# Matmuls whose results nobody reads, gate scores with tokens as the moving operand, and a third normalisation done tile by tile, in a graph attention + mixture-of-experts kernel on one core

## What is computed

```python
# graph layer, on the normalised input
h   = layer_norm(node_feature, ln1_g, ln1_b)
q, k, v = (h @ Wqkv + bqkv) split, 8 heads of 64
a   = einsum(q[src], k[dst]) + dist_attn + path_attn
sa  = exp(a - segment_max(a, dst)[dst]) / segment_sum(...)[dst]
agg = segment_sum(v[src] * sa, dst)
h1  = node_feature + agg @ Wo + bo
h2  = layer_norm(h1, ln2_g, ln2_b)
x   = x + h1 + gelu(h2 @ W1 + b1) @ W2 + b2
# mixture of experts, on the third normalisation of x
xt     = layernorm(x)
shared = silu(xt @ sw1) * (xt @ sw3) @ sw2
scores = xt @ gate_w.T                      # 8 experts
idx    = top_k(scores + biases, 2);  p = sigmoid(top_k(scores, 2)) normalised
out    = x + shared + sum over the two experts of p * (silu(xt @ w1[e]) * (xt @ w3[e])) @ w2[e]
```

## Time and profile before

| | |
|---|---|
| device time, median of 3 executions | 819.65 us (819.62 to 820.09) |
| device time of the profiled execution | 819.31 us |
| its span from first to last instruction | 817.9 us |
| mean granted TensorE clock | 0.967 of full speed |
| PE busy | 758.2 us, 93% of the span |
| DVE, ACT, POOL busy | 547.0, 461.2, 221.3 us |
| DMA | 92.46 MB, mean 113 GB/s |

### The profile page before, as it was taken

One profiled execution on the slowest core, in us unless ns is written; L12 is line 12 of the kernel. 1 busy time (PEld: TensorE's weight loads), 2 busy tenths in 40 slices (PEclk: granted clock), 3 DMA queues, 4 the chain that ended last, 5 costly groups with the idle time before them and its releaser, 6 DMA issues. The chain is left out here.

```text
span 817.9 us, 13330 instructions
## 1 busy us (share of the span) xinstructions
PE 758.2 (93%) x4993; PEld 632.5 (77%) x4993; DVE 547.0 (67%) x937; ACT 461.2 (56%) x748; POOL 221.3 (27%) x156
## 2 busy tenths in 40 slices
PE   3998899999999979799999599979999999999994
PEld 2664688788878865599998499868889888888893
DVE  6637997979797844444222644357888788888855
ACT  5254686868687752733342523227667667676640
POOL 9340786868687750000000001300000000000022
PEclk9999899999999999899999689989999999999997
DMA  8231920000000007000000700956666776767214
GB/s 267 81 49 54 323 56 2 1 2 1 2 1 2 2 2 264 5 1 1 1 1 1 232 1 19 375 191 231 220 222 214 234 242 222 260 225 229 80 56 153
DMA packets 66460, 92.46 MB, mean 113 GB/s; under 512 B 6723, under 2 KB 44197, under 8 KB 65877
## 3 DMA queue, kind: packets, MB, share of 16 engines
q1 hardware_dynamic: 64149, 85.77, 32.1%
q0 software_dynamic: 2240, 5.76, 2.3%
HBM read 80.69 MB, written 10.82 MB: 112 GB/s over the span
## 5 line engine op out<-in xcount | busy, mean ns | idle before, releaser
L682 POOL TENSOR_TENSOR bias_exp_hi<-edge_exp_hi,mask 128x640 fp32r<-128x640 f32 x40 | 98.0, 2450 | 72.6 <-PE ps L828 32.3
L1806 PE MATMUL ps<-xT,w_hi 128*128 128x480 f32 (+7 forms) x512 | 111.1, 339 | 3.7 <-DVE w_lo L1621 3.6
L1806 PEld LDWEIGHTS ps<-xT,w_hi 128*128 128x128 f32 x512 | 83.2, 191 | 10.2 <-issue 3.8
L1621 DVE TENSOR_TENSOR w_lo<-weights_far,w_hi 128x1024 fp32r<-128x1024 f32 x64 | 78.0, 1219 | 3.1 <-ACT w_hi L1721 2.7
L1607 POOL DMA_INDIRECT weights_far<-slot_results,gate x5 | 5.2, 1034 | 272.2 <-DMA slot_results<-weights_near 271.0
L1808 PEld LDWEIGHTS ps<-xT,w_lo 128*128 128x128 f32 x512 | 74.0, 191 | 1.7
L1808 PE MATMUL ps<-xT,w_lo 128*128 128x240 f32 (+7 forms) x512 | 74.9, 269 | 0.0
L828 PE MATMUL ps<-onehot,bias_exp_hi 128*128 128x314 f32 x400 | 69.5, 320 | 5.5 <-POOL bias_exp_hi L682 5.0
L1721 ACT ACTIVATE w_hi<-weights_far 128x1024 fp32r<-128x1024 f32 x64 | 67.2, 1051 | 0.0
L828 PE MATMUL ps<-onehot,bias_exp_lo 128*128 128x314 f32 x400 | 65.3, 310 | 0.0
L828 PEld LDWEIGHTS ps<-onehot,bias_exp_hi 128*128 128x128 f32 x400 | 59.4, 193 | 6.5 <-POOL bias_exp_hi L682 5.2
(11 more groups left out here) (270 smaller groups left out, 1650.8 us busy)
## 6 DMA issues: line engine op xcount, KB each, us to landing
weights_far<-in_L_ffn_w SPq DMA_DIRECT2D x64, 512.0 KB, 5.4
weights_near<-in_L_ffn_w SPq DMA_DIRECT2D x32, 512.0 KB, 3.6
weights_near<-in_L_gnn_W SPq DMA_DIRECT2D x1, 4096.0 KB, 14.4
weights_near<-in_L_gnn_Wqkv SPq DMA_DIRECT2D x3, 1024.0 KB, 7.8
weights_ff<-in_L_gnn_W SPq DMA_DIRECT2D x1, 3072.0 KB, 13.3
weights_lo_shared<-in_L_ffn_sw SPq DMA_DIRECT2D x6, 512.0 KB, 7.7
weights_near<-in_L_ffn_sw SPq DMA_DIRECT2D x6, 512.0 KB, 6.3
slot_rows<-zeros SPq DMA_DIRECT2D x1, 2944.0 KB, 26.4
```

Source lines behind the costliest of these rows:

```text
L682: pool.tensor_tensor(to.rearrange("p t (h d) -> p t h d", h=H), e[:, b, :, :].unsqueeze(3).broadcast_to([P, CT, H, BN]), m.unsqueeze(2).br ...
L1621: dve.tensor_tensor(to[1], raw_rest[n] if v == V else raw[u][n], to[0], ALU.subtract)\
L1806: pe.matmul(both(bank, cap), w[u % 2][0][:, c, cut], xT(r)[:, c, :, :], start=c == 0, stop=False)
```

## The change

A helper `keep_awake` issues plain fp32 matmuls 128x512 of the identity and `iota_n` into a PSUM bank that nothing reads before it is written anew. It is called at six places of the PE stream: 3 at the end of `projections`; 3 at the start of attention (behind the load of its branch value, ahead of `sums(0, 0)`); 3 ahead of `turn(39)`, behind a wait for the 39th reciprocal; 2 and 1 ahead of feed-forward's `turn(3)` and `turn(4)`; 1 ahead of each tile's turning in the third normalisation and 2 behind the last; 4 between the experts' `turn(0)` and their first `up`.

In feed-forward the first half of the columns waits for three low parts only, the second half for all five. The gate weights are loaded and turned at the block's start. `down(14)` and `down(15)` are done for tiles 0 to 3 first and then both for tile 4. SP loads the first quarter of the shared expert's weights into `w_near` once W1 has been used. The third normalisation moves to the end of this block and goes tile by tile, the normalised row on ACT, and the high and low parts are read from PSUM. PE does the first half of `up(0)` of the shared expert there, ahead of the barrier. The routing block starts with the second half; the scores then are eight matmuls with the gate's eight columns as weights and 314 tokens moving, copied by ACT to SBUF and turned to token rows by five small matmuls in the middle of `up(1)`. The rest is passing buffers, renaming and freeing semaphores.

```diff
+def keep_awake(pe, bank, ident, filler, times):
+    for _ in range(times):
+        pe.matmul(bank[:, 0:D], ident[:, :], filler[:, 0:D], start=True, stop=True)
...
             back(2)
+            keep_awake(pe, psum[0], ident, iota_n, 3)
...
+            keep_awake(pe, psum[4], ident, iota_n, 3)
             for b in range(NB):
                 sums(b, 0)
...
                 if b:
                     turn(b - 1)
+            pe.wait_ge(inv_ready, NB - 1)
+            keep_awake(pe, psum[0], ident, iota_n, 3)
             turn(NB - 1)
             weighted_sums(NT - 1)
...
+            sp.dma_start(gate_row, gate_w).then_inc(vec_in, 16)
+            sp.dma_start(bias_r, biases.rearrange("(a n) -> a n", a=1).broadcast_to([P, EX])).then_inc(vec_in, 16)
...
+            sp.wait_ge(split_lo, 2 * MC - 1)
+            for to, frm in ((moe1, sw1[:, 0:UW].rearrange("(c p) n -> p c n", p=P)),
+                            (moe3, sw3[:, 0:UW].rearrange("(c p) n -> p c n", p=P)),
+                            (moe2, sw2[0:UW, :].rearrange("(c p) n -> p c n", p=P))):
+                sp.dma_start(to, frm).then_inc(moe_in, 16)
...
+            def moe_measure(t):
                 n = own_rows(t)
                 dve.wait_ge(y_ps, t + 1)
                 dve.tensor_tensor(xs[0:n, t, :], xs[0:n, t, :], psum[t][0:n, :], ALU.add).then_inc(y_sb, 1)
+                dve.wait_ge(y_sb, t + 1)
+                o.link(dve.bn_stats(stats[:, t, :], xs[:, t, :]))
+                dve.bn_aggr(mv[:, t, :], stats[:, t, :]).then_inc(moe_mv, 1)
+            def moe_factors(t):
+                dve.wait_ge(moe_std, t + 1)
+                o.link(dve.reciprocal(rstd[:, t:t + 1], std[:, t:t + 1]))
+                dve.scalar_tensor_tensor(out=below_mean[:, t:t + 1], in0=mv[:, t, 0:1], scalar=-1.0,
+                                         in1=rstd[:, t:t + 1], op0=ALU.mult, op1=ALU.mult).then_inc(moe_scale, 1)
+            def moe_low(t):
+                dve.wait_ge(moe_hi, t + 1)
+                cut = slice(t * P, (t + 1) * P)
+                dve.tensor_tensor(rows_T[1][:, :, cut], psum[t][:, :].rearrange("p (c n) -> p c n", c=DC),
+                                  rows_T[0][:, :, cut], ALU.subtract).then_inc(moe_lo, 1)
+            for t in range(NT):
+                moe_measure(t)
+                if t:
+                    moe_factors(t - 1)
+                if t >= 3:
+                    moe_low(t - 3)
+            moe_factors(NT - 1)
+            for t in range(2, NT):
+                moe_low(t)
...
+            for t in range(NT):
+                moe_root(t)
+                if t:
+                    moe_row(t - 1)
+                if t > 1:
+                    moe_high(t - 2)
+            moe_row(NT - 1)
+            act.preload_act_table_set("silu_and_others")
+            moe_high(NT - 2)
+            moe_high(NT - 1)
...
             def turn(t):
+                if t >= NT - 2:
+                    pe.wait_ge(columns_ready, 1)
+                    keep_awake(pe, psum[7], ident, iota_n, NT - t)
                 pe.wait_ge(rows, t + 1)
...
-            pe.wait_ge(rows_lo, NT)
...
+                    if m == 0:
+                        pe.wait_ge(rows_lo, NT if half else 3)
...
-            down(MC - 1)
+            down(MC - 2, range(NT - 1))
+            down(MC - 1, range(NT - 1))
+            down(MC - 2, range(NT - 1, NT))
+            down(MC - 1, range(NT - 1, NT))
+            pe.wait_ge(u_sb, 2 * MC)
+            for t in range(NT):
+                keep_awake(pe, psum[7], ident, iota_n, 1)
+                pe.wait_ge(moe_rows, t + 1)
+                for c in range(DC):
+                    last = pe.transpose(psum[t][:, c * P:(c + 1) * P], vs[:, t, c * P:(c + 1) * P], ident[:, :])
+                last.then_inc(moe_turned, 1)
+            keep_awake(pe, psum[7], ident, iota_n, 2)
+            pe.wait_ge(moe_lo, 3)
+            for n in range(2):
+                pe.wait_ge(moe_split_lo, n + 1)
+                for i, (wp, xp) in enumerate(passes):
+                    for c in range(DC):
+                        last = pe.matmul(up_bank[n][:, 0:SH], w1s[n][wp][:, c, :], rows_T[xp][:, c, 0:SH],
+                                         start=i == 0 and c == 0, stop=i == 2 and c == DC - 1)
+                last.then_inc(moe_a_ps, 1)
...
-            up(0)
-            for t in range(NT):
+            up(0, range(1, 2))
+            pe.wait_ge(moved, NT)
+            for half in range(2):
                 for c in range(DC):
-                    last = pe.matmul(score_ps[:, t * EX:(t + 1) * EX], hT[:, c, t * P:(t + 1) * P], gate_t[:, c, :],
+                    last = pe.matmul(psum[half][0:EX, 0:SH], gate_t[:, c, :], hT[:, c, half * SH:(half + 1) * SH],
                                      start=c == 0, stop=c == DC - 1)
-            last.then_inc(sc_ps, 1)
+            last.then_inc(sc_rows_ps, 1)
+            def scores():
+                pe.wait_ge(sc_rows_sb, 1)
+                for t in range(NT):
+                    n = own_rows(t)
+                    last = pe.transpose(score_ps[0:n, t * EX:(t + 1) * EX],
+                                        sc_rows.rearrange("e a n -> e (a n)")[:, own_cut(t)], ident[0:EX, 0:EX])
+                last.then_inc(sc_ps, 1)
             for m in range(1, HS):
-                up(m)
+                up(m, then=scores if m == 1 else None)
...
             turn(0)
+            keep_awake(pe, psum[4], ident, iota_n, 4)
             for v in range(V):
```

More of the change, by code:

```diff
@@ L886, in feed_forward @@
         parts = ("hi", "lo")
-        rows_T = [sb(f"ff_rows_{part}", [P, DC, NP]) for part in parts]
-        w1s = [[sb(f"ff_w1_{part}{i}", [P, DC, P]) for part in parts] for i in range(2)]
         w2s = [[sb(f"ff_w2_{part}{i}", [P, D]) for part in parts] for i in range(4)]
@@ L1067, in _, with down @@
             turn(NT - 1)
-            pe.wait_ge(rows_lo, NT)
-            def down(m):
+            pe.wait_ge(gate_ready, 1)
+            def down(m, tiles=range(NT)):
                 pe.wait_ge(h_lo, m + 1)
                 pe.wait_ge(split_lo, 2 * m + 2)
-                for t in range(NT):
+                for t in tiles:
                     for i, (hp, wp) in enumerate(passes):
@@ L1108, in routing @@
         parts = ("hi", "lo")
-        w1s, w3s = ([[sb(f"sh_{w}_{part}{i}", [P, DC, P]) for part in parts] for i in range(2)] for w in ("w1", "w3"))
+        w1s, w3s = ([pairs[n], [sb(f"sh_{w}_{part}", [P, DC, P]) for part in parts]] for n, w in enumerate(("w1", "w3")))
         w2s = [[sb(f"sh_w2_{part}{i}", [P, D]) for part in parts] for i in range(4)]
@@ L1254, in chunk @@
                 dve.tensor_tensor(hid[m % 2][1], h32[m % 2], hid[m % 2][0], ALU.subtract).then_inc(h_lo, 1)
-            for n in range(3):
-                weights_lo(0, n)
+            weights_lo(0, 2)
             chunk(0)
@@ L1370, in _, with up @@
         def _(pe):
[L1371 to L1383 removed]
             passes = ((0, 0), (0, 1), (1, 0))
             pe.wait_ge(rows_lo, NT)
[L1387 to L1388 removed]
+            def up(m, halves=range(2), then=None):
+                for half in halves:
+                    if half and then:
+                        then()
                     for n in range(2):
```

186 lines of the change are left out of this document (102 added, 84 removed).

## The result

The changed kernel takes **806.85 us** (median of 4 executions, 805.94 to 808.53) against 819.87 us of the kernel before beside it (819.62 to 820.72, 4 executions). The ratio is 0.9842, with a 95% interval of 0.9822 to 0.9861: faster by 1.4 to 1.8%. The forecast was 808.5, the range 804.8 to 814.5.

What follows compares the result with a forecast made beforehand. PE is busy 93% of the span, so time goes where it waits or runs at half clock. 1.6 - 1.6 - 2.7 - 4.8 - 1.7 - 1.9 = -11.1 from 819.31 gives 808.2, plus 0.3 is 808.5 us; range 804.8 to 814.5.

Steps and rivals of the forecast that it cites:

- A: Projections to attention: the barrier waits for three unread matmuls, with no gain from a warm clock; +1.6 us.
- B: End of attention: behind three unread matmuls the last weighted sums take 4.60 instead of 6.21; -1.6 us.
- C: Feed-forward's start: first half of the columns runs after three low parts; turning the gate weights adds near 0.6; -2.7 us.
- D: Third normalisation: tile by tile, earlier start, up(0) done sooner and warm, two unread matmuls costing 1.76; -4.8 us.
- E: Experts' first unit: behind four unread matmuls its four pairs take 5.3 instead of 7.2; -1.9 us.
- S: Gate scores to places(): scores -0.9, five turnings +0.8, warm up(1) -2.0, later picks +0.4; -1.7 us.
- signs of being wrong: Low clock in the watched windows, PE waiting over 1 us at places(), or E's gain gone 20 us later.
- I take no gain: Attention's start: a warm clock gives nothing, since PE's 4.1 us at half clock are covered by DVE's one-hots.
- The rule against D: Third normalisation: transposes don't count as PE activity, so the clock falls there; the prediction went by the trace instead.
- rival 1: Clock falls in the third normalisation or its neighbour: +3 to +7, about 813; rivals 1 to 3 together 0.33.
- rival 2: New scores leave the clock low and up(1) cold: +2 to +5, about 812; rivals 1 to 3 together 0.33.
- rival 3: Idle of 1.88 before the experts lowers the clock: E about +1.5, total 812; rivals 1 to 3 together 0.33.

Runs made afterwards that it cites:

- no_a: The changed kernel without the six unread matmuls around attention's start; 807.24 us, ratio 0.9831.
- old_order: The changed kernel with feed-forward's first half waiting for all five low parts again and the last two downs tile by tile; 812.0 us, ratio 0.9906.
- no_unread: The changed kernel without its 23 unread matmuls, everything moved staying moved; 809.77 us, ratio 0.986.
- fewer_and_moved: The changed kernel without attention's six and the third normalisation's last two unread matmuls, one of the experts' four moved ahead of the block change; 803.11 us, ratio 0.9797.
- fewer_no_d: fewer_and_moved without the five unread matmuls ahead of each tile's turning in the third normalisation; 805.79 us, ratio 0.982.
- old_scores: The changed kernel with the gate scores as before, 20 matmuls with eight columns moving; 809.87 us, ratio 0.9875.
- no_e: The changed kernel without the four unread matmuls ahead of the experts' first unit; 809.99 us, ratio 0.9868.
- before_unread: The kernel before with the same 23 unread matmuls at the corresponding places and nothing moved; 820.7 us, ratio 0.9997.
- no_a_two_in_e: The changed kernel without the six unread matmuls around attention's start and with two instead of four ahead of the experts' first unit; 806.9 us, ratio 0.9833.
- fewer_with_a: fewer_and_moved with the six unread matmuls around attention's start put back; 808.17 us, ratio 0.9853.
- fewer_no_c: fewer_and_moved without the three unread matmuls ahead of feed-forward's last two turnings; 804.87 us, ratio 0.9805.

## Why the prediction was right, term by term

The mechanisms of A, B, C and D held; E's did not, S's held in part, and 1.97 us came from a place that the sum didn't have. That the terms add up to within 0.2 of the forecast is partly luck: E's miss of 1.4 is made up by 0.8 and 0.7 too little in D and S.

| term | predicted | measured | where |
|---|---|---|---|
| A | +1.6 | +1.53 | DVE's gap 3.10 for 1.58, no_a |
| B | -1.6 | -1.61 | L878 |
| C | -2.7 | -2.33 | to feed-forward's end, less B |
| D | -4.8 | -5.57 | to the scores |
| S | -1.7 | -2.36 | to `places()` |
| E | -1.9 | -0.54 | to the fifth group |
| between `places()` and `turn(0)` | 0 | -1.97 | not foreseen, cause open |
| scatter at start and end | 0 | +0.63 + 1.32 | |

Of the signs that the prediction names, the clock (1.00 through 300 to 345 and 450 to 490), L860's 4.6 and the 18.4 to the scores came; DVE's first step of attention came 1.52 later behind its projections (2.16 in all); the first pair of the experts took 1.71 (537.77 to 539.48) and not 1.3. None of the signs of being wrong came: `places()` waited for less than 0.3, and what E gained was still there at the gather (235.79 for 235.81).

**A and B** came as worked out. The sentence "the barrier has to wait for them" held, and so did "I take no gain".

**C.** The mechanism is right, and old_order shows the split wait to be more than all of it: 3.13 of gain, against which 0.8 is lost elsewhere in the stretch (366.27 - 1.61 is 364.66, and old_order has 365.46). The turning of the gate weights, put at 0.6, lies there. The second half starts at 338.80 [1.58], so its 24th matmul ends at 340.56, against 342.7 before; with the shift of 0.55 that A, B and the start leave, that is 2.7 earlier, the term as forecast. `down(0)` starts 2.6 and feed-forward ends 2.3 earlier; the last 0.3 spread over 100 us and weren't followed. The three unread matmuls, for which I took a warm first chunk, are worth 0.11.

**D.** The sum of DVE's steps gave `rows_lo` 3 at 9.5 behind PE's last matmul; it was 8.6 (457.11 - 448.52). A tile with its factors took DVE 1.77 (from 446.62 to 448.38 and on), where I had 1.65 + 0.36 = 2.01; the factors took 0.13 and 0.16 and overlapped their neighbours. The wait for ACT was 0.98 where I had 0.8. "Two unread matmuls cost 1.76" proved right to 0.04 (1.72). That they were worth their price was not tested in my text, and they were not: left out, the clock stays. And all of D's gain is there without any unread matmul: no_unread has 18.33 for the 23.99 of before. Its low clock costs 1.6 against the 16.70 of fewer_and_moved, far from the 5.4 put at four cold groups, because it lies mostly under the turnings (455.0 to 461.8).

The rule against D: the clock stayed at 1.00 through 448.5 to 458.0, while PE alternated turnings and unread matmuls, so rival 1 did not happen. The Trainium skill (TensorE: Matmul & The Clock Gate, Part 4: PE-mode transpose) says that transposes do not count as PE-busy in the same way. The forecast drawn from it, a fall in D, is contradicted by this row; that turnings alone did not hold the clock in fewer_no_d fits the rule but also the mere idle between them, so these runs don't settle it.

**S.** -0.9 + 0.8 - 2.0 + 0.4 were, by the timelines: scores 4.32 for 5.59, -1.27; the five turnings +0.40; `up(1)` 7.24, in two pieces, for 9.00, -1.76; from there to `places()` +0.27. The price of the scores was mis-sized, and misread besides: 20.8 us for 34 matmuls is 0.61 each and not 0.59, and eight took 4.32. Most of the gain would have come without the new scores (old_scores gets 1.60 of the 2.36): the clock falls under the old ones there too, but for 3.4 us. Under the new ones and `up(1)` it stayed at 1.00, so rival 2 did not happen.

**E** failed as rival 3 had it: behind the idle of 1.87 the clock fell, at about 533.6, the four ran mostly cold, and the first pair came 0.98 later than it does without them (5.62 behind `turn(0)` for 4.64). That the first `up` could start at once behind them, at 548.47, and that four pairs would take 5.3 are the steps that were off: +0.98 and +0.37 (5.67 for the four pairs). The rival's price, "-1.9 to about +1.5", was too dark: the clock was low for 3.4 of the 5.3 us, not all of them. The term also hides what the four are worth: against the changed kernel without them they bring 1.1 (12.36 in no_e, 12.48 in no_unread), not 0.54. In before the low stretch began 1.8 behind `turn(0)`, in no_e and no_unread 3.0 to 3.2, so more of it lay under the pairs.

Rival 1's argument that "each low stretch was preceded by more idling than D leaves" was not true of the stretch at 477.6, ahead of which PE was fully occupied, as the prediction's first paragraph says itself.

**Not foreseen** were 1.97 us in the shared expert. Before, PE waits 1.78 at 522.57, for ACT, which stood idle for 8.13:

```profile
513.34 0.62 ACT L1349 ACTIVATE sh_w_hi<-weights_lo_shared 128x512 fp32r<-128x512 f32 x1
522.08 0.43 ACT L1362 ACTIVATE sh_gated<-ps 128x314 f32<-128x314 f32 x1 [8.13 <-PE ps L1399]
```

The matmuls that L1362 reads began at 515.40 and their twelve were done by 517.2, so 4.8 of it have no cause that the profile shows. The kernel before with unread matmuls has it too (7.23 idle, 0.89 on PE). The change did not remove it: ten of the eleven versions of the changed kernel have an idle of ACT of 5.1 to 6.6 at the same line of the program, and only after has none over 3.9. There it costs PE 0 or at most 0.26. So the -1.97 is for 1.78 the length of one stall in one trace of before; what makes the stall, and how long it is in other executions of before, is open.

The six terms add up to -10.9 where -11.1 was forecast, with E worth 1.4 less and D and S 0.8 and 0.7 more than worked out. Outside them the -1.97 stands against +1.95 of scatter in this profile; the medians differ by 13.0, and -10.9 - 1.97 = -12.9 is near that. This would account for the median 1.65 under the forecast, but only one execution of each kernel was traced, so it is not shown.

## What to carry to other kernels

Unread matmuls pay only where PE waits anyhow and the clock would fall: here five of 23 cost 1.53 and 1.72 (three delayed a barrier, two stood in front of ready work), three more behind that barrier gave nothing back, and taking out these eight and moving one of the rest won 3.7 us more than the whole set. Put one where PE is idle under another engine's last steps ahead of a block change, so that those behind it run warm. Moving work into a wait came first: the moved work and the new scores brought 10 us (no_unread), a split wait alone 3.13, while the unread matmuls brought 2.9 as they were first placed and 6.7 as they were placed last (809.77 to 803.11). Of the third normalisation's 5.66 no run tells apart tile by tile, the early gate weights and the half of `up(0)` ahead of the barrier.

## What was not expected of the hardware

- Same stream, two clocks. `places()` is ten fp32 matmuls with eight columns moving, 2.2 us, and behind it the clock is low for 3.4 us in six of the thirteen profiles (before_unread, no_a, no_a_two_in_e, old_scores, fewer_with_a, fewer_no_c), and in seven not, though PE's instructions around it are the same in the versions of the changed kernel. It costs some 1.6 us (that stretch is 53.1 to 53.8 with it and 51.6 to 52.3 without, in versions of the changed kernel), and executions of one kernel differ so as well: the four of fewer_no_c took 803.01 and 804.08 us at a mean granted clock of 0.99 and 805.65 and 805.8 at 0.985. Medians of versions that differ by one call can therefore differ by more than the call. The Trainium skill (TensorE: Matmul & The Clock Gate, Part 1: The HAM clock gate) says that the number of cold matmuls varies between runs of one kernel; the four executions of fewer_no_c agree.
- PE fully occupied does not keep the clock up: under the old scores, entered warm, it fell at about 470.4, with PE busy for 3.40 of the 3.40 us ahead of it (466.90 to 470.30).
- A plain fp32 matmul 128x512 at full clock takes 1.02 alone, two take 1.88 and three 2.74 to 2.84, so each further one adds 0.86 to 0.96, and leaving two out saved 1.72. The low stretches between 26 us and the last stage lasted 3.4 or 6.8 us in all thirteen profiles.
